# MoE and Mamba in five chunks (256, 512, 512, 512, 256 tokens) instead of four of 512, on one Trainium2 core

## The reference

```python
# MoE: every expert works on every token; weights is zero but for the top 2
probs = softmax(xf @ w_router)
weights = top-2 of probs, others 0
h = gelu(einsum('te,ieh->tih', xf, w1) + b1)        # 8 experts, 128 -> 512
out = einsum('tih,ihe->tie', h, w2) + b2            # 512 -> 128
x = x + gb * sum(out * weights)
# Mamba: D_INNER 256, 16 states, over the 2048 tokens in order
x_val = silu(conv4(x @ W_in_x.T)); z = x @ W_in_z.T
dt = softplus(x[:, :64] @ W_dt.T + b_dt); Bm = x @ W_B.T; Cm = x @ W_C.T
h = exp(dt * A) * h + (dt * x_val) * B_t            # h: 256 x 16, carried from token to token
y = sum over states(h * C_t); x = x + ga * ((y * silu(z)) @ W_out.T)
# last part
x = x + gb * (layernorm(x) mixed by one 128x128 matrix + bias)
```

## Time and profile before

| | us |
|---|---|
| median of 3 runs | 672.67 |
| lowest and highest | 669.57, 674.6 |
| the profiled execution | 669.75 |
| span in its profile | 667.7 |
| busy: PE, DVE | 515.8, 431.0 |
| busy: ACT, POOL | 369.2, 355.1 |

### The profile page before, as it was taken

How to read it: one execution, slowest core, us unless ns; L and a number is a source line. 1 busy time by engine, 2 the same in 40 slices (tenths; PEclk the granted TensorE clock), 3 DMA queues, 4 the chain that set the end, 5 groups by cost and what they waited for, 6 DMA issues and landing times.

```text
span 667.7 us, 6946 instructions
## 1 busy us (share of the span) xinstructions
PE 515.8 (77%) x2368; PEld 354.4 (53%) x2368; DVE 431.0 (65%) x727; ACT 369.2 (55%) x510; POOL 355.1 (53%) x224
## 2 busy tenths in 40 slices
PE   4578587559589889998878798788888768756673
PEld 4365455335477778676646557456557533333322
DVE  5658878832532333128886687696587698889972
ACT  1434142134454464769887888687788446745301
POOL 3127785633501011205878774978774857548551
PEclk9989897879789899999989999799899779978996
DMA  8500000000000000300101100112100111101100
GB/s 319 193 1 0 0 1 1 1 0 0 1 0 1 1 1 0 129 1 32 64 32 65 32 32 33 63 48 64 34 33 32 58 52 65 64 32 63 47 1 16
DMA packets 12562, 26.93 MB, mean 40 GB/s; under 512 B 1968, under 2 KB 7472, under 8 KB 12272
## 3 DMA queue, kind: packets, MB, share of 16 engines
q1 hardware_dynamic: 11952, 25.57, 10.9%
q10 hardware_dynamic: 576, 0.92, 0.4%
HBM read 25.31 MB, written 1.18 MB: 40 GB/s over the span
## 4 chain that ended last, share of the span: by engine, by line
PE 41%; DVE 27%; ACT 15%; issue 8%; POOL 7%; DMA 1%; ACTq 0%; POOLq 0%; DVEq 0%
PE pO L1183 9%; DVE Hs L724 8%; DVE pCT L711 5%; PE pH L1221 4%; ACT gel L934 4%; DVE S L619 4%; PE pH L1171 3%; PE pY L1265 3%; ACT dA L946 3%; PE pY L1258 3%; ACT L946 2%; DVE pH L618 2%; PE pH L1173 2%; POOL Zod L364 2%; POOL ZS L377 2%
## 5 line engine op out<-in xcount | busy, mean ns | idle before, releaser
L1183 PEld LDWEIGHTS pO<-w_e,gel 128*128 128x128 f32 x1024 | 129.3, 202 | 11.4 <-issue 9.8
L1183 PE MATMUL pO<-w_e,gel 128*128 128x128 f32 x1024 | 130.2, 285 | 0.0
L724 DVE TENSOR_TENSOR_SCAN Hs<-dA,HL,pCT 128x512 f32<-128x512 f32 x96 | 117.7, 1268 | 9.1 <-issue 4.0
L934 ACT ACTIVATE gel<-pH,b_e 128x512 f32<-128x512 f32 x128 | 86.4, 687 | 64.6 <-PE pH L1173 63.8
L711 DVE TENSOR_TENSOR pCT<-u,pB 128x1024 f32<-128x1024 f32 x64 | 78.4, 1225 | 41.7 <-PE pB L1246 40.7
L364 POOL TENSOR_TENSOR Zev<-Hs,Crow 128x1024 f32<-128x1024 f32 x32 | 75.6, 2363 | 54.8 <-DVE Hs L724 54.5
L946 ACT ACTIVATE dA<-dt,a_neg 128x512 f32<-128x512 f32 x128 | 81.8, 710 | 26.7 <-DVE Hs L724 26.5
L1171 PE MATMUL pH<-h2h,w_e1h 128*128 128x512 f32 x128 | 57.8, 452 | 19.2 <-ACT gel L934 17.6
L695 DVE SCALAR_TENSOR_TENSOR X<-pO,wts,X 128x128 f32<-128x128 f32 x128 | 35.9, 343 | 50.9 <-PE pO L1183 50.9
L364 POOL TENSOR_TENSOR Zod<-Hs,Crow 128x1024 f32<-128x1024 f32 x18 | 42.5, 2363 | 40.3 <-DVE Hs L724 40.3
L425 POOL TENSOR_TENSOR ZA<-Qsb,S 128x1024 f32<-128x1024 f32 x16 | 37.9, 2372 | 35.7 <-DVE S L619 32.8
(11 more groups left out here) (196 smaller groups left out, 974.9 us busy)
## 6 DMA issues: line engine op xcount, KB each, us to landing
Crow<-c_rows SPq DMA_DIRECT2D x32, 512.0 KB, 3.7
w_e<-in_w_e SPq DMA_DIRECT2D x2, 2048.0 KB, 10.7
X<-in_x SPq DMA_DIRECT2D x4, 256.0 KB, 6.8
out<-h2T SPq DMA_DIRECT2D x4, 256.0 KB, 2.2
S<-in_w_mod ACTq DMA_DIRECT2D x2, 384.0 KB, 4.6
w_cx<-in_conv_row SPq DMA_DIRECT2D x1, 512.0 KB, 9.5
w_f<-in_w_f SPq DMA_DIRECT2D x2, 128.0 KB, 5.8
b_e<-in_b_e SPq DMA_DIRECT2D x1, 256.0 KB, 13.3
```

The source lines that it names most:

```text
L724: vec.tensor_tensor_scan(Hs[:, 2 * o + d, 0:w], dA[:, 4 * (p % 2) + 2 * o + d, 0:w], pU[:, d, 0:w], HL[:, d, n:n + 1] if c else 0.0, ALU.m ...
L934: nc.scalar.activation(gel[:, n % NG, 0:w], pH[n % 2][:, 0:w], ACT.Gelu_apprx_tanh, bias=b_e1[:, NK * e + k:NK * e + k + 1]).then_inc(s["m ...
L1183: ins = mm(pO[:, j * P:(j + 1) * P], gel[:, n % NG, j * P:(j + 1) * P], w_e2[:, NK * (g % E) + k, :], start=(k == 0 and j == 0), stop=(k = ...
```

## The change

WIDTHS becomes 256, 512, 512, 512, 256. So there are five chunks, 40 experts' rounds and 40 pairs, of which sixteen each are 256 tokens wide. AHEAD stays 13: experts 0 to 12 run with no pair, pairs 0 to 26 beside experts 13 to 39, pairs 27 to 39 with no expert. ALONE becomes 26 by its formula. The routing of chunks 1 to 3 stays at rounds -13, -10 and -7; that of chunk 4 starts at round 0 (without the new condition it would be -4). h2h and h2l are stored by token, one row of 2048, instead of by chunk.

```diff
-WIDTHS = [512, 512, 512, 512]
+WIDTHS = [256, 512, 512, 512, 256]
 NL = len(WIDTHS)
 ALONE = (NL * E - AHEAD) // 2 * 2
...
-        h2h = sb("h2h", [P, NL, TC], F32R)
-        h2l = sb("h2l", [P, NL, TC], F32R)
+        h2h = sb("h2h", [P, T], F32R)
+        h2l = sb("h2l", [P, T], F32R)
...
+        def span_of(t, c):
+
+            return t[:, sum(WIDTHS[:c]):sum(WIDTHS[:c + 1])]
+
...
                 for q in range(1, NL):
-                    at = k - (p + AHEAD - 3 * (q - 1))
+                    at = k - (p - (3 * (q - 1) - AHEAD if q < 4 else 0))
...
-                mm(pH[n % 2][:, 0:w], w_e1h[:, g % E, part], h2h[:, c, 0:w], start=True, stop=False)
+                mm(pH[n % 2][:, 0:w], w_e1h[:, g % E, part], span_of(h2h, c), start=True, stop=False)
```

More of the change, by code:

```diff
@@ L450, in route @@
                 pool.wait_ge(s["ln_evac"], E0[c])
-                pool.tensor_tensor(h2l[:, c, 0:w], h2T[:, 0:w], h2h[:, c, 0:w].bitcast(F32),
+                pool.tensor_tensor(span_of(h2l, c), h2T[:, 0:w], span_of(h2h, c).bitcast(F32),
                                    ALU.subtract).then_inc(s["h2_lo"], 1)
@@ L885, in _ @@
                     ln_apply(0)
-                    ln(h2T[:, 0:WIDTHS[0]], 0, 2, 1, h2h[:, 0, 0:WIDTHS[0]])
+                    ln(h2T[:, 0:WIDTHS[0]], 0, 2, 1, span_of(h2h, 0))
             def route(c, b):
@@ L949, in turned @@
             def turned(c, which, b):
-                ln([h2T, h4T, h4T][which][:, 0:WIDTHS[c]], c, 2 + 2 * which, b, None if which else h2h[:, c, 0:WIDTHS[c]])
+                ln([h2T, h4T, h4T][which][:, 0:WIDTHS[c]], c, 2 + 2 * which, b, None if which else span_of(h2h, c))
             def run(stages, places):
@@ L1170, in up @@
                     pe.wait_ge(s["set_pool"], 5 + 2 * (g // (E // NC)))
-                mm(pH[n % 2][:, 0:w], w_e1h[:, g % E, part], h2h[:, c, 0:w], start=True, stop=False)
-                mm(pH[n % 2][:, 0:w], w_e1h[:, g % E, part], h2l[:, c, 0:w], start=False, stop=False)
-                mm(pH[n % 2][:, 0:w], w_e1l[:, g % E, part], h2h[:, c, 0:w], start=False, stop=True).then_inc(s["moe_h"], 1)
+                mm(pH[n % 2][:, 0:w], w_e1h[:, g % E, part], span_of(h2h, c), start=True, stop=False)
+                mm(pH[n % 2][:, 0:w], w_e1h[:, g % E, part], span_of(h2l, c), start=False, stop=False)
+                mm(pH[n % 2][:, 0:w], w_e1l[:, g % E, part], span_of(h2h, c), start=False, stop=True).then_inc(s["moe_h"], 1)
             def down(g, k):
```

## The result

The changed kernel takes 700.97 us (median, 696.38 to 706.37), the kernel before 672.58 beside it (669.57 to 674.60): a ratio of 1.043, 95% interval 1.038 to 1.048. The direction was forecast, the size was not: 685 was said, with a range up to 698.

A forecast was written before the change was run, and what follows sets the result against it. The bounding engine changes by stage (PE lone experts, DVE lone pairs, none above 83% in mixed rounds). Terms -4-20-6-10-5+17+6+41-7 = +12 took the span from 667.7 to 679.7, the median to 685; range 666 to 698.

The forecast's parts named there:

- less 1.1 a round: Pairs 19 to 26: narrow experts take 1.1 us off each full mixed round (GELUs 0.9, half a hidden part), 101.7 to 93.
- 1.3 for the clock: Experts 0 to 8: 1.3 us added for PE's slower clock, 60.7 worked out to 62 taken.
- the 19.3 worked out: Experts 0 to 8: three rounds of lone narrow experts with one chunk's routing take 19.3 us, where 27.3 before.
- rival C: Slower still: narrow experts' and narrow rounds' matmuls at 1.2 GHz, +13, 698; scan at 0.95, +8; above 692, chance 0.19.
- The 2.0 for a GELU held up by ln_x: Lone narrow experts: the next chunk's ln_x, ready 5.9 us after a round begins, delays GELU by 2.0 of a 3.5 round.
- a third of one tail's 13 goes: Pairs 8 to 18: chunk 0's tail, half as wide, saves a third of its 13 us; term -5, bounds -8 and 0.
- The head, -4 forecast: Before the first expert: chunk 0's own routing, in series there, shrinks with its width, -4 us, bounds 0 and -6.
- The scan at 0.70: DVE's scan of 256 elements takes 0.70 us, if its element costs two product steps; bounds 0.61 and 0.95.
- the round of 7.4 to 8: Pairs 0 to 7: GELU to GELU beside narrow pairs takes 7.4 to 8 us, ACT's sequence being 7.4.
- already in the terms: Whole kernel: 98 ACT table loads instead of 77, 21x1.28 = 27 us, counted within the stage terms, nothing added.
- A (the narrow side hides): Faster: in the 16 rounds with one narrow side it hides wholly, under 157 us together; 665 total, chance 0.13.
- B: A draw: losses are real, but routing is better covered (54 for 62) and chunk 3's tail hides; 673, chance 0.22.

The follow-up runs named there:

- one table: Kernel before with GELU replacing exponential, softplus and silu (other values), 72 fewer table loads: 651.14 us, ratio 0.967; same in the changed kernel, 93 fewer: 671.25, 0.996.
- the two edits: Changed kernel with GELU replacing exponential, softplus and silu, and PE's next B row moved earlier in rounds 19 to 26: 664.82 us, ratio 0.991.
- the early row: Changed kernel with PE's B row for the next pair ahead of total, stations and way down, rounds 19 to 26: 698.53 us, ratio 1.038.
- the repetition: The changed kernel timed and profiled a second time, no edit: 700.95 us, ratio 1.040.

## Why the prediction was right or wrong

**Pairs 19 to 26, 92.7 forecast, 99.7 measured.** The starting value was right: eight full mixed rounds, 101.7. The step that failed is "less 1.1 a round", which took off the GELUs' shorter time and half a hidden part as if they lay on the path. They gave 0.25 a round, and the runs with twice and a third of the hidden matmuls (99.9, 98.0) show that the hidden parts are hardly on it. Halving PE's time at 1.2 GHz gave 1.2 us, and PE's sums in place of POOL's gave nothing. What sets the stage is, as far as the runs go, the coupling of engines that work in order: the decays behind the GELUs and two table loads on ACT, the next row behind stations and the way down on PE. Removing one wait exposed the next: 4.2 us for the row, 8.0 for the loads, 13.5 for both.

The stage lies 24.0 us above the kernel before. Of the 13.5, the kernel before would gain 2.8 too (75.7 becomes 72.9 with one table), so the two edits account for 10.7, and 13.3 remain (86.2 for 72.9). Half of these are work: DVE is busy for 73.5 us, against 66.9 in the kernel before with one table. The rest, 6.7, are waits in which PE's hidden parts, POOL's sums and the early row's own wait for DVE all have a part; no run took any of them away alone, and the cause of this rest stays open.

**Experts 0 to 8, 62 forecast, 66.5 measured.** The term that failed is "1.3 for the clock", which was too small as far as the traces tell. The first routing set took 19.8, near the 19.3 worked out; its router matmuls took 1.08, and its slow way down (3.64) ended with DVE's routing operations beside it. The second and third, whose router matmuls took 1.88, lie 2.6 each above the working; in both a way down of 3.61 instead of 1.95 is part of the chain that ended last. In all, 23.4 of the 66.5 us ran at 1.2 GHz against 10.2 of 82.0 before. So the mechanism of rival C was there, at most at a third of its price (4.5 for 13). No run shows how much of the 4.5 is the clock's: with twice the hidden work and a mean clock of 0.93 the stage was as long. The 2.0 for a GELU held up by ln_x was right (PE waits 1.76 there).

**Pairs 8 to 18, -5 forecast, -1.2 to -1.4 measured.** The step "a third of one tail's 13 goes" failed. Pairs 11 to 18 are the same in both kernels (101.7 and 101.9); at pairs 8 to 10 the narrower tail gave 1.4 (38.1 becomes 36.7). So the tail's steps seem to lie largely beside other waits in a mixed round; no run tested that.

**The head, -4 forecast.** From the last attention scan to the first GELU it gave 46.6 - 43.4 = 3.2. But the unchanged attention part moved by 1.6 to 4.9 us between profiles, which one profile of each kernel can't tell from an effect of the change, and which the sum had at nothing.

**Right within 1.4 us** were experts 9 to 12, pairs 0 to 7 (chunk 4's routing included), 27 to 31 and 32 to 39, and in the repetition the end. The scan at 0.70, taken between 0.61 and 0.95, and the pair at 4.3 were exact, and eight narrow pairs cost 40.2 of 41. For pairs 0 to 7 only the total was right: the round of 7.4 to 8 in its working came once in eight. The cost of table loads as "already in the terms" was right in kind: 21 of them are 27 us of ACT's time and some 7 of the kernel's.

**The rivals.** A (the narrow side hides) fell with 184 us for its sixteen rounds, where it needed 157. B fell with it. C had about the right total by luck: the scan was not slow, the clock was worth 4.5 at most where C had 13, and the largest miss lay at pairs 19 to 26, where C had nothing.

The median lies 16 above the forecast. By the repetition the stages lie 19.2 above it (7.0, 4.4 and 3.6 from the three terms, 2.2 from the head, 2.0 from the rest), and 3.1 come back, as 5.0 had been put between span and median where 1.9 were. In two of the three terms, pairs 19 to 26 and 8 to 18, work was taken off that had lain beside something else.

## What to carry to other kernels

Splitting work into smaller pieces halves what an engine does in a round, but not the round, when the round is a ring of waits between engines that work in order; price such a round by a measured round of the same kinds of work, and take nothing off it without a row that shows the work on the path. Before adding or removing work, look at what stands in an engine's order ahead of the instruction that another engine waits for: here one call moved past the station work gave 1.0%, while removing two thirds of the narrow experts' hidden matmuls gave 1.7 us at pairs 19 to 26 and nothing among the lone experts. A saving whose wait is replaced by another (row, then decays) is worth the difference only, so price two such chains together, and ask which wait the edit itself will make.

## What the runs showed of the hardware that was not expected

- The granted clock followed the amount of work at equal time: 270, 332 and 426 matmuls in the same stage took 67.3, 66.5 and 66.4 us, at a mean of 0.75, 0.82 and 0.93.
- Whether time at 1.2 GHz costs anything depends on the stage: 17.0 us less of it gave 1.2 us at pairs 19 to 26, and 12.8 us more of it came with 5.2 us more at pairs 32 to 39.
- An ACT_TABLE_LOAD of 1.28 us, with the next work 1.30 after its start where nothing else held it up, was worth 0.31 to 0.32 us of the kernel's time on average over 72 and 93 loads taken away.
- The same attention code took 133.2 to 138.5 us until its last scan in the profiled executions of these kernels, with 25.5 to 42.9 us of it at 1.2 GHz and not in proportion: where the slow phases fall differs from run to run. A stage that the change doesn't touch is to be compared first.
